# Cross-attention and expert mixing on one core: folded matrix in halves, and a first step with PSUM pairs and orders of its own

## What is computed

```python
# cross attention, 8 heads of 64
q = einsum('oc,bcn->bon', Wq, layernorm(x))       # softmax over the 64 of a head, / 8
kv = einsum('oc,bcn->bon', Wkv, context)          # k: softmax over the 1024 columns; v as it is
ctx = einsum('bhdn,bhen->bhde', k, v)
out = einsum('bhde,bhdn->bhen', ctx, q)
out = Wout @ out + b_out;  out = (out - mean) * rsqrt(var + 1e-5) * g
x = x + out
# expert mixing, 64 experts of rank 16, the top 16 of them for each row
G = softmax of the 16 highest of layernorm(x) @ Wr.T, 0 elsewhere
x = x + 2 * (((layernorm(x) @ A.T) * G) @ B)
```

## Time and profile before

| | us |
|---|---|
| median of 3 runs | 1824.46 (1823.97 to 1826.51) |
| the profiled execution's own time | 1825.84 |
| its span, first to last instruction | 1824.1 |
| step 0 of the attention part, PE's first to last product of it | 14.4 to 36.3 |
| first product of step 1 on PE | 43.32 |

### The profile page before, as it was taken

How to read it: one execution, slowest core, us unless ns; L and a number is a source line. 1 busy time by engine, 2 the same in 40 slices (tenths; PEclk the granted TensorE clock), 3 DMA queues, 4 the chain that set the end, 5 groups by cost and what they waited for, 6 DMA issues and landing times.

```text
span 1824.1 us, 29121 instructions
## 1 busy us (share of the span) xinstructions
PE 1768.9 (97%) x9586; PEld 1526.4 (84%) x9586; DVE 1475.0 (81%) x1979; ACT 1040.0 (57%) x1270; POOL 1206.5 (66%) x581
## 2 busy tenths in 40 slices
PE   4999999999999999999999889999999999999998
PEld 3888888888888888888888788999999999999987
DVE  6899999999999999999999976777777777777751
ACT  4888888888888888888888743222222222222110
POOL 3878787887878788787878736555555555555531
PEclk9999999999999999999999999999999999999999
DMA  6243333424233333424234354444444444444441
GB/s 156 61 104 79 83 88 89 92 75 106 72 86 92 85 89 84 98 74 105 74 84 124 107 174 150 162 162 162 161 161 159 159 160 158 158 161 161 147 140 49
DMA packets 294477, 213.78 MB, mean 117 GB/s; under 512 B 215008, under 2 KB 256480, under 8 KB 294432
## 3 DMA queue, kind: packets, MB, share of 16 engines
q1 hardware_dynamic: 280784, 189.60, 35.8%
q0 software_dynamic: 4608, 16.78, 3.3%
q10 hardware_dynamic: 9040, 6.82, 1.3%
HBM read 147.06 MB, written 70.25 MB: 119 GB/s over the span
## 4 chain that ended last, share of the span: by engine, by line
PE 82%; DVE 6%; issue 6%; POOL 3%; ACT 2%; DMA 0%; DVEq 0%; ACTq 0%; SPq 0%; POOLq 0%
PE ps L52 24%; PE ps L54 23%; PE ps L53 23%; PE ps L1442 6%; PE ps L1432 5%; DVE k_min L990 2%; DVE m_lo L1020 1%; POOL rstd_c L559 1%; ACT m_hi L714 1%; POOL o_blk L565 1%; POOL hT_lo L574 1%; ACT ek L681 0%; DMA ek<-in_L_xattn_Wkv 0%; DVE w_ra_lo L1030 0%; POOL xT_lo L569 0%
## 5 line engine op out<-in xcount | busy, mean ns | idle before, releaser
L544 POOL TENSOR_TENSOR eq<-eq,q_inv 128x1024 f32<-128x1024 f32 x128 | 242.4, 1900 | 161.2 <-DVE q_inv L986 161.2
L548 POOL TENSOR_TENSOR kT_lo<-kT,kT_hi 128x1024 fp32r<-128x1024 f32 x128 | 305.9, 2400 | 35.3 <-ACT kT_hi L663 32.0
L569 POOL TENSOR_TENSOR xT_lo<-work,xT_hi 128x1024 fp32r<-128x1024 f32 x31 | 74.0, 2388 | 290.6 <-ACT xT_hi L766 290.6
L52 PE MATMUL ps<-w_ra_hi,xT_hi 128*128 128x384 f32 (+1 forms) x768 | 251.0, 327 | 3.1 <-POOL xT_lo L569 1.6
L53 PE MATMUL ps<-w_ra_lo,xT_hi 128*128 128x384 f32 (+1 forms) x768 | 250.2, 326 | 0.0
L54 PE MATMUL ps<-w_ra_hi,xT_lo 128*128 128x384 f32 (+1 forms) x768 | 250.2, 326 | 0.0
L52 PE MATMUL ps<-w_b_hi,hT_hi 128*128 128x512 f32 x496 | 196.0, 395 | 0.0
L54 PE MATMUL ps<-w_b_hi,hT_lo 128*128 128x512 f32 x496 | 194.1, 391 | 0.0
L53 PE MATMUL ps<-w_b_lo,hT_hi 128*128 128x512 f32 x496 | 193.6, 390 | 0.0
L670 ACT ACTIVATE qh<-ps,k_inv 128x1024 fp32r<-128x1024 f32 x128 | 142.9, 1116 | 71.3 <-PE ps L1432 65.4
L559 POOL TENSOR_TENSOR rstd_c<-var_c,minus_half 128x32 f32<-128x32 f32 x32 | 173.5, 5422 | 10.2 <-DVE var_c L1056 10.2
(11 more groups left out here) (160 smaller groups left out, 4713.7 us busy)
## 6 DMA issues: line engine op xcount, KB each, us to landing
x_sb<-in_x SPq DMA_DIRECT2D x64, 512.0 KB, 4.5
ctx_sb<-in_ctx SPq DMA_DIRECT2D x32, 512.0 KB, 3.9
ctx_hi<-in_ctx POOLq DMA_DIRECT2D x32, 512.0 KB, 4.0
ctx_blk<-in_ctx SPq DMA_DIRECT2D x512, 32.0 KB, 2.3
attention_out<-o_sb SPq DMA_DIRECT2D x32, 512.0 KB, 2.7
o_sb<-attention_out SPq DMA_DIRECT2D x32, 512.0 KB, 4.8
x_turn<-x_blk SPq DMA_DIRECT2D x31, 512.0 KB, 2.6
work<-x_turn SPq DMA_DIRECT2D x124, 128.0 KB, 2.8
```

Of the source, the lines that this page charges most:

```text
L52: pe.matmul(out, stat_hi, mov_hi, start=first, stop=False)
L544: pool.tensor_tensor(v, v, per_row(q_inv[:, i, :], 2 * HEADS, DH), ALU.mult).then_inc(q_normed, 1)
L548: pool.tensor_tensor(kT_lo[:, i % 2, :, :], kT[:, i % 2, :, :], kT_hi[:, i % 2, :, :].bitcast(F32), ALU.subtract).then_inc(kT_lo_ready, 1)
```

## The change

Six things are changed.

1. **Folded matrix by halves, in every step.** `folded_hi` and `folded_lo` take two of the four chunks at a time, so there are four instructions of 64x256 on ACT and four on DVE in place of two of 64x512. `fold` signals after each half. `add_output(b, 0)` waits for the first half only, `add_output(b, 2)` for the second.
2. **The context's hi part, in every step.** `context_hi` is no longer a transfer that POOL issues, but a copy by ACT from `ctx_sb`, placed between `query_hi(s - 1, 2)` and `exp_queries(s, 2)`.
3. **Pairs of the first step.** In step 0 the eight K and Q jobs use `FIRST_PAIR`, so that all three pairs are used.
4. **Orders of the first step.** PE, ACT, DVE and POOL each have an order of their own for step 0. On ACT and POOL, x of batch 1 is normalised right after the first exponential, not near the end; `projection` and `centre_projection` come earlier.
5. **x of batch 0 in two halves** of 512 columns, so that queries 0 and 1 need only the first; and query weights are turned, split and signalled before the key weights.
6. **SP** waits for x of batch 0 to land before it issues anything behind the two weight loads.

```diff
+FIRST_PAIR = dict(Q0=2, K0=0, Q1=1, K1=2, Q2=0, K2=1, Q3=2, K3=0)
...
             load_x(0, 0)
-            sp.dma_start(wq_raw, Wq.rearrange("(j p) c -> p j c", p=P)).then_inc(qk_loaded, 16)
-            sp.dma_start(wk_raw, Wkv[0:HD, :].rearrange("(j p) c -> p j c", p=P)).then_inc(qk_loaded, 16)
+            sp.dma_start(wq_raw, Wq.rearrange("(j p) c -> p j c", p=P)).then_inc(wq_loaded, 16)
+            sp.dma_start(wk_raw, Wkv[0:HD, :].rearrange("(j p) c -> p j c", p=P)).then_inc(wk_loaded, 16)
+            sp.wait_ge(x_loaded[0], 16)
             each_step(sp, step)
...
+                elif edge and s == 0:
+                    rstd_x(1)
+                    x_lo(1, 1)
+                    for i in range(2):
+                        norm_queries(0, 0, i)
+                    context_lo(1, 1)
+                    context_turned_lo(0)
+                    norm_queries(0, 0, 2)
...
                     if X_:
                         rstd_x(s + 1)
-                        context_hi(s + 1, 1 - par)
...
+            def context_hi(b, p):
+                act.wait_ge(ctx_loaded[p], 8 * (b - p) + 16)
+                wait_for(act, k_made, CH * (b - 1))
+                act.copy(ctx_hi[p][:, :], ctx_sb[p][:, :]).then_inc(ctx_hi_ready, 1)
...
-            def folded_hi(b, h):
-                r = slice(h * DH, (h + 1) * DH)
-                act.wait_ge(m_made, b + 1)
+            def folded_hi(b, half):
+                jj = slice(2 * half, 2 * half + 2)
+                act.wait_ge(m_made, 2 * b + half + 1)
                 wait_for(act, o_part, 4 * b)
-                act.copy(m_hi[r, :, :], folded[r, :, h, :]).then_inc(m_hi_ready, 1)
+                for h in range(2):
+                    r = slice(h * DH, (h + 1) * DH)
+                    act.copy(m_hi[r, jj, :], folded[r, jj, h, :]).then_inc(m_hi_ready, 1)
...
+            def first_x():
+
+                act.wait_ge(shift_ready, 1)
+                for n, (normed, made) in enumerate(((half_normed, half_hi_ready), (xn_ready, xn_hi_ready))):
+                    c = slice(n * BANK, (n + 1) * BANK)
+                    act.activation(xn[:, c], x_sb[:, 0, c], ACT.Identity, bias=shift[:, 0:1],
+                                   scale=rstd[:, 0:1]).then_inc(normed, 1)
+                    act.wait_ge(normed, 1)
+                    act.copy(xn_hi[0][:, c], xn[:, c]).then_inc(made, 1)
...
                 if QT:
                     query_hi(s - 1, 1 - par, 2)
+                if X_:
+                    context_hi(s + 1, 1 - par)
                 if Q:
                     exp_queries(s, par, 2)
...
                 dve.tensor_copy(wq_hi[:, :], wqT).then_inc(qk_hi_ready, 1)
+                dve.wait_ge(qk_hi_ready, 1)
+                dve.tensor_tensor(wq_lo[:, :], wqT, wq_hi[:, :].bitcast(F32), ALU.subtract).then_inc(qk_lo_ready, 1)
+                first_x_lo(0, half_hi_ready, half_lo_ready)
+                dve.wait_ge(qk_turned, 2)
                 dve.tensor_scalar(wk_hi[:, :], wkT, -1.0, None, ALU.mult).then_inc(qk_hi_ready, 1)
                 dve.wait_ge(qk_hi_ready, 2)
-                dve.tensor_tensor(wq_lo[:, :], wqT, wq_hi[:, :].bitcast(F32), ALU.subtract).then_inc(qk_lo_ready, 1)
-                dve.wait_ge(xn_hi_ready, 1)
...
-                    pe.wait_ge(m_lo_ready, 2 * b + 2)
+                    pe.wait_ge(m_lo_ready, 4 * b + 2)
                     pe.wait_ge(t_lo_ready, b + 1)
+                if j == 2:
+                    pe.wait_ge(m_lo_ready, 4 * b + 4)
...
+            def first_step():
+
+                turn_weights()
+                queries(0, 0, 0, True)
+                queries(0, 0, 1, True)
+                keys(0, 0, 0, True)
+                keys(0, 0, 1, True)
+                centre_projection()
+                queries(0, 0, 2, True)
+                keys(0, 0, 2, True)
+                queries(0, 0, 3, True)
+                keys(0, 0, 3, True)
```

More of the change, by code:

```diff
@@ L222, in xattn_ffn @@
         kT_lo_ready, q_normed = sem("kT_lo_ready"), sem("q_normed")
-        ctx_hi_loaded = [sem(f"ctx_hi_loaded{i}") for i in range(2)]
+        ctx_hi_ready = sem("ctx_hi_ready")
         ctx_lo_ready = sem("ctx_lo_ready")
@@ L229, in xattn_ffn, with pair, slot, flat @@
                      "QT": q_lo_ready}
-        def slot(job):
-            return ps[:, PAIR[job]]
-        def flat(job):
-            return slot(job).rearrange("p a b -> p (a b)")
+        def pair(job, b=None):
+            return FIRST_PAIR[job] if isinstance(b, int) and b == 0 and job in FIRST_PAIR else PAIR[job]
+        def slot(job, b=None):
+            return ps[:, pair(job, b)]
+        def flat(job, b=None):
+            return slot(job, b).rearrange("p a b -> p (a b)")
         acc = ps[:, 3]
@@ L252, in wait_slot @@
                     n, back = n + len(RING), back + 1
-                if PAIR[RING[n]] != PAIR[job]:
+                if pair(RING[n], s - back if edge else None) != pair(job, s if edge else None):
                     continue
@@ L876, in last_step @@
                 weight_hi(8)
+            def first_x():
[7 more added lines that the diff above has]
+            def first_step():
+                exp_queries(0, 0, 0)
+                negate_mean(1)
+                shift_x(1)
+                norm_x(1, 1)
+                x_hi(1, 1)
+                exp_queries(0, 0, 1)
+                exp_keys(0, 0, 0)
+                exp_keys(0, 0, 1)
+                exp_queries(0, 0, 2)
+                context_hi(1, 1)
+                projection()
+                exp_keys(0, 0, 2)
+                context_turned_hi(0)
+                exp_queries(0, 0, 3)
+                exp_keys(0, 0, 3)
             def step(s, par, edge):
@@ L880, in step @@
                     last_step(s, par)
+                    return
+                if edge and s == FIRST_STEP:
+                    negate_mean(0)
+                    shift_x(0)
+                    first_x()
+                    context_hi(0, 0)
+                    return
+                if edge and s == 0:
+                    first_step()
                     return
@@ L919, in step @@
                     exp_keys(s, par, 2)
-                if edge and s == 0:
-                    projection()
                 if M:
@@ L945, in _, with first_x_lo @@
         def _(dve):
+            def first_x_lo(n, hi_ready, lo_ready):
+                c = slice(n * BANK, (n + 1) * BANK)
+                dve.wait_ge(hi_ready, 1)
+                dve.tensor_tensor(xn_lo[0][:, c], xn[:, c], xn_hi[0][:, c].bitcast(F32), ALU.subtract).then_inc(lo_ready, 1)
             def weights():
@@ L1015, in weighted_lo, with folded_lo @@
                 dve.tensor_tensor(t_lo[:, :], acc[:, 0], t_hi[:, :].bitcast(F32), ALU.subtract).then_inc(t_lo_ready, 1)
-            def folded_lo(b, h):
-                r = slice(h * DH, (h + 1) * DH)
-                dve.wait_ge(m_hi_ready, 2 * b + h + 1)
-                dve.tensor_tensor(m_lo[r, :, :], folded[r, :, h, :], m_hi[r, :, :].bitcast(F32),
-                                  ALU.subtract).then_inc(m_lo_ready, 1)
+            def folded_lo(b, half):
+                jj = slice(2 * half, 2 * half + 2)
+                for h in range(2):
+                    r = slice(h * DH, (h + 1) * DH)
+                    dve.wait_ge(m_hi_ready, 4 * b + 2 * half + h + 1)
+                    dve.tensor_tensor(m_lo[r, jj, :], folded[r, jj, h, :], m_hi[r, jj, :].bitcast(F32),
+                                      ALU.subtract).then_inc(m_lo_ready, 1)
             def turn_context(b, p):
@@ L1272, in first_step @@
                 stats_x(1, 1, 0)
+                max_queries(0, 0)
+                shift_queries(0, 0, 0)
                 stats_x(1, 1, 1)
                 mean_x(1)
-                for i in range(4):
-                    max_queries(0, i)
-                    shift_queries(0, 0, i)
-                    if i == 2:
-                        turn_context(0, 0)
-                        sum_queries(0, 0, 0)
-                        invert_sums(0, 0)
-                    if i == 3:
-                        sum_queries(0, 0, 1)
-                        invert_sums(0, 1)
-                    min_keys(0, 0, i)
+                max_queries(0, 1)
+                shift_queries(0, 0, 1)
+                min_keys(0, 0, 0)
+                sum_queries(0, 0, 0)
+                invert_sums(0, 0)
+                min_keys(0, 0, 1)
+                sum_queries(0, 0, 1)
+                invert_sums(0, 1)
+                max_queries(0, 2)
+                shift_queries(0, 0, 2)
+                turn_context(0, 0)
+                min_keys(0, 0, 2)
+                max_queries(0, 3)
+                shift_queries(0, 0, 3)
                 sum_queries(0, 0, 2)
                 invert_sums(0, 2)
+                min_keys(0, 0, 3)
             def step(s, par, edge):
@@ L1417, in queries @@
                 wait_slot(pe, f"Q{i}", s, edge)
-                if i == 0:
+                if edge and s == 0:
```

(4 more changed lines are left out.)

52 lines of the change are left out of this document (25 added, 27 removed).

## The result

The changed kernel takes 1809.52 us (median of 4 runs, 1808.30 to 1812.12) against 1824.51 for the kernel before in the same comparison: a ratio of 0.9918, 95% interval 0.9901 to 0.9935. The forecast was 1806.5, in a range of 1798 to 1815. Timed again with five runs, it took 1809.03 (ratio 0.9921, 0.9908 to 0.9935). One of the six executions of s2_ring_pairs ran in a second, slower state of the chip (1954.04 us at a granted clock of 0.85) and is left out of its median.

A forecast was written before the change was run, and what follows sets the result against it. PE, busy for 97% of the span, was taken as the bound, leaving only its stops and low clock. First step 11.4 us plus folded matrix 6.6 made 18.0 us, so a median of 1806.5 us, range 1798 to 1815.

The forecast's parts named there:

- Start: Opening of the first step: PE's first product at 9.25 us in place of 14.39, 5.1 us earlier.
- DVE's row of work: First step, first maximum to last minimum on DVE: 20.8 us of work, ending at 33.7, 6.3 us earlier.
- The one wait foreseen: First step: queries 2 wait for the exponential of keys 0; half-speed products cost 1.3 us, 0.6 reaching DVE.
- The turn: Passage to step 1: PE turns batch 0's keys from 34.85 in place of 46.2, 11.35 us earlier.
- The 0.9 us for a full clock at the turn: Turn to step 1: PE's eight transposes at 2.4 GHz would give 0.9 us more, left out of the sum.
- The folded matrix: Each of about 30 steps: halves remove PE's wait for m_lo, gaining 0.22 us a step, 6.6 us in all.
- The wait that takes its place: Each step: PE's wait on m_lo would be replaced by a shorter one on kT_lo, behind POOL's chain.
- The context copy: Each step: ACT's added 1.05 us of work just fills its idle time before qh, costed at nothing.
- 1 (0.5 us a step): Rival: POOL's chain does not hold PE, so the folded matrix gives its full 0.5 us; 1798 us, chance 0.16.
- 2 (nothing): Rival: the folded matrix's halves give nothing or cost up to 0.2 us a step; 1813 to 1819 us, chance 0.16.
- 3: Rival: the first step gives only 6 to 8 us, through late transfers or DVE stalls; 1810 to 1812, chance 0.14.
- 4: Rival: the context copy lies on the path and the kernel gets slower, 1844 us at the full 1.05; chance 0.04.

The follow-up runs named there:

- s2_ring_pairs: The changed kernel with the ring's bank pairs in the first step too, in place of FIRST_PAIR; 1818.12 us, ratio 0.9975.
- s1: The changed kernel without SP's wait for x of batch 0; 1809.30 us, ratio 0.9922.
- s4: The changed kernel with x of batch 0 normalised, rounded and subtracted whole, not in halves; 1810.90 us, timed once.
- e1: The kernel before with the folded matrix in halves and nothing else; 1819.32 us, ratio 0.9970.
- e6: The kernel of e5 with other bank pairs for queries 2, keys 2 and keys 3 in the first step; 1804.70 us, ratio 0.9900.
- e1b: The changed kernel with the folded matrix whole and POOL's context transfer again from step 1 on; 1814.09 us, ratio 0.9950.
- e5: The changed kernel with ACT, in each full step, normalising x ahead of exp_keys 2 and rounding the turned context last; 1807.48 us, ratio 0.9902.
- e3: The changed kernel with the context's hi part fetched by POOL's transfer again from step 1 on; 1808.16 us, ratio 0.9914.
- e4: The changed kernel with ACT's context copy made twice in every step from 1 on; 1823.28 us, ratio 0.9994.
- e2: The changed kernel with the folded matrix whole again; 1813.36 us, ratio 0.9939.
- s3: The changed kernel with x of batch 1 normalised late in the first step again, on ACT and POOL; 1813.35 us, ratio 0.9949.

## Why the prediction held, and where it was off

**Start: the place right, part of the size luck.** First product 9.35 for 9.25, first maximum 12.29 for 12.1. The key weights were early, as assumed, but not because SP waits: without its wait they still came in time (s1). Of the 5.0 us by which the first product moved, 1.4 are x in halves (s4). Another 1.6 are luck: in e1, with the start of the kernel before, PE's transposes began at 7.53 and the first product came at 12.79, against 9.12 and 14.39 in the trace that the forecast was read from. The 2.0 us left go with the query weights being turned and split by themselves; this was not tried alone.

**DVE's row of work: right.** Its end was put at 33.7 and was 33.86. The one wait foreseen, queries 2 behind the exponential of keys 0 at half speed, is there, with 0.96 us on DVE in place of 0.6. e6 shows that this term came from the choice of pairs, and e1b that it isn't the same in every execution: there the products ran at 2.4 GHz at first, and DVE did not wait.

**The turn: right, by 0.4 us late.** Predicted 34.85, came 35.25, released by the exponential. The 0.9 us for a full clock at the turn, which I did not count, came: 0.50 from 43.3 to 47.7 before, 1.00 now. 11.4 was forecast and 11.6 measured at A, but against the first step of e1 it is 9.8. The medians say the same: before and after differ by 15.0 and, timed again, by 14.2; less the 4.6 us of the steps behind A, 9.6 to 10.4 is left for the first step, where e1b has 9.2. So about 1 to 2 us of the 11.4 were a late landing in the one execution that it was read from, and the close match at A is luck in that part. How often the weights land late was not measured. The median came out 3.0 us above the forecast, about what this and the folded matrix (2.0) add up to.

**The folded matrix: the mechanism right, the term too large.** The `m_lo` wait went and shorter ones took its place, but a step gained 0.15 us and not 0.22, 4.6 us in all and not 6.6. The mis-sized term is what halves cost ACT: I had 0.11 us of fixed time per extra piece, from the 64x512 eviction and a 128x1024 cast. The piece of 64x256 took 363 ns:

```profile
L731 ACT CAST m_hi<-ps 64x256 fp32r<-64x256 f32 x128 | 46.5, 363 | 2.3
```

With 574 for 512 elements that leaves 152 ns fixed, so 0.30 us for two pieces, and 0.36 as the chain shows it (1.53 for 1.17). My 128x1024 row was a cast from SBUF and said little on reads of PSUM.

The Trainium skill's table (VectorE: DVE Perf Modes, section on the TRN2 errata) gave 0.36 us for such a copy by estimate; the trace agrees, with 363 ns. The section's advice on tile size is about sources in SBUF, and this source is PSUM, for which the table has its own column. The gain of 0.15 a step that the prediction worked out from that figure was met as well, but it charges all of the loss to POOL's chain, and the next paragraph shows that a part of it lies elsewhere.

**The wait that takes its place: half right.** I named `kT_lo` behind POOL's chain alone. That wait of PE's weight loads grew from 6.9 to 9.7 us, 0.10 us a step, and e5, which eases POOL's chain, got 0.10 back. But 6.1 us, 0.22 a step, now stand at K3's pair, which DVE's `ql` must free, and `ql` waits 0.54 us for `qh` behind ACT's longer pieces (0.34 before). No run eases this wait alone, so that it holds the remaining 0.25 of the half microsecond is what the trace suggests and is not shown. I had asked only who waits for POOL, not whose pair DVE frees behind `folded_lo`.

**The context copy: right.** Nothing for one (e3), 0.50 us a step for a second (e4).

**Rivals.** 1 (0.5 us a step) falls: even with POOL's chain eased 0.25 is reached (e5). 2 (nothing) falls by e1 and e2. 3 falls: no engine waits for a transfer in step 0 behind the first weights. 4 is real but does not show with one copy.

## What to carry to other kernels

Splitting an eviction from PSUM to release its reader sooner paid 0.15 us here for a wait of half a microsecond, because the fixed part of each piece goes to everyone queued behind it: follow that lateness over every engine's queue and over every buffer that they free. At a start-up, look at which stop of the matmul engine is longest and which buffer causes it; the new bank pairs of the first step were worth more at A (8.8 us) than the early x (4.7) or x in halves (1.4), and giving one late job yet another pair brought 1.1 more and kept the clock. Before filling an engine's idle time, read that time in the trace: here 1.55 us held a 1.04 us copy at no cost, and a second copy cost half of its length in each step. And read the start from more than one trace before: one execution can carry a late transfer that the change did not cause and will not cure.

## What the runs showed of the hardware

Behind the same stop, 3.58 us in one kernel and 3.60 in another with the same code there, PE's clock went from 2.4 to 1.2 GHz in both, but in one within the stop and in the other some 1.2 us after it, while products were running. It came back between 26.1 and 26.5 in the one, between 25.7 and 26.0 in the other (products 0.23 apart again). The length of the stop alone does not tell what comes behind it. After stops of up to 1.73 us in e6 the clock stayed at the full level, and after 5.66 (s3) the products ran at the half. Between these it went both ways: after 2.58 us in the kernel before (at 27.82) the granted clock was 0.52, and s2_ring_pairs has four stops of about the same length with three outcomes.

```profile
14.68 0.79 PE L52 MATMUL ps<-wq_hi,xn_hi 128*128 128x512 f32 x1 [2.57 <-DVE eq L1035]
...
31.00 0.50 PE L52 MATMUL ps<-ctx_hi,wk_hi 128*128 128x512 f32 x1 [2.58 <-DVE eq L1035]
```

Behind the stop at 14.68 the products followed at 0.43. Behind those at 31.00 and 35.40 (2.74 us) they followed at 0.23 to the last. Behind the one at 22.69 (2.55 us) three were fast and the others slow. From 14.70 to 17.00 the window all the same shows a granted clock of 1.00, so the spacing of the products has to be read beside that number. A kernel with such a stop can differ by it from one execution to the next, here by 0.84 us; how much of the scatter of the times this makes was not measured.

The part of the program behind B, which no kernel here changed, took 816.4 to 821.0 us. A gain of 0.10 us a step could be read between two marks in the trace, where equal kernels agreed to 0.03 a step, and not from the medians.
